# Delta rule: one is added to the gate's tanh, and the gate product is done on GpSimd instead of VectorE, with new step orders on all engines

## The reference, cut to what matters

```python
def step(S, inp):
    qt, kt, vt, at, bt = inp
    err = jnp.einsum('bhvk,bhk->bhv', S, kt) - vt
    S = at[..., None, None] * S - bt[..., None, None] * err[..., None] * kt[:, :, None, :]
    o = jnp.einsum('bhvk,bhk->bhv', S, qt)
    return (S, o)
...
o = (o - mu) * jax.lax.rsqrt(var + 1e-05) * ln_w + ln_b
g = jax.nn.sigmoid(x @ Wg).reshape(B, T, H, DV)
o = (o * g).reshape(B, T, H * DV)
return o @ Wo
```

## Time and profile before

| what | value |
|---|---|
| median of three runs | 1885.67 us (1882.06 to 1886.81) |
| the profiled execution | 1887.38 us, of which the span is 1885.6 us |
| TensorE busy | 1781.6 us, 94% of the span |
| VectorE busy | 1529.9 us, 81% |
| ScalarE busy | 1286.9 us, 68% |
| GpSimd busy | 941.3 us, 50% |
| mean granted TensorE clock | 0.977 of full speed |

### The profile page before, as it was taken

The page is one execution under the profiler, slowest core; times in us unless marked ns, Lnnn a source line. Parts: engine busy times, 40 slices in busy tenths (PEclk is TensorE's granted clock), DMA queues, the critical chain, the costliest instruction groups (busy, mean ns, idle before and its releaser), DMA issues.

```text
span 1885.6 us, 49242 instructions
## 1 busy us (share of the span) xinstructions
PE 1781.6 (94%) x19366; PEld 1315.9 (70%) x19366; DVE 1529.9 (81%) x2561; ACT 1286.9 (68%) x2850; POOL 941.3 (50%) x1890
## 2 busy tenths in 40 slices
PE   8889999999899889999999999999999999999687
PEld 4733333332688767888888888888888888887576
DVE  6699999993466567989989999899899898998455
ACT  2068888889342357778777777787777777777553
POOL 1134344445223244666566566666666566565233
PEclk9989999999899999999999999999999999999889
...
DMA packets 74133, 78.61 MB, mean 42 GB/s; under 512 B 13168, under 2 KB 60784, under 8 KB 73904
## 3 DMA queue, kind: packets, MB, share of 16 engines
...
## 4 chain that ended last, share of the span: by engine, by line
PE 38%; ACT 14%; DVE 9%; issue 4%; POOL 1%; POOLq 0%; ACTq 0%; DVEq 0%
PE ps L1530 10%; PE ps L1678 5%; PE ps L1560 4%; DVE d_acc L1833 3%; PE ps L1660 3%; ACT d_kq L1717 3%; ACT d_tt L1769 2%; PE ps L1648 2%; PE ps L1654 2%; PE ps L1630 2%; ACT d_acc L1701 2%; PE ps L1637 2%; DVE d_o_g L1910 2%; PE ps L2008 1%; ACT d_ty L1766 1%
## 5 line engine op out<-in xcount | busy, mean ns | idle before, releaser
L1833 DVE SCALAR_TENSOR_TENSOR d_acc<-ps,d_par,d_acc 128x1023 f32<-128x1023 f32 (+2 forms) x288 | 366.1, 1271 | 25.7 <-ACT d_acc L1701 25.5
L601 ACT ACTIVATE a_prob<-ps 128x512 f32<-128x512 f32 (+2 forms) x640 | 309.3, 563 | 99.1 <-PE ps L567 93.9
L1530 PE MATMUL ps<-x1p,d_wh 128*128 128x512 f32 x1024 | 358.7, 431 | 7.1 <-DVE d_acc L1833 7.1
L623 DVE TENSOR_REDUCE a_mx<-ps 128x2 f32<-128x1024 f32 (+2 forms) x320 | 336.5, 1112 | 34.9 <-PE ps L551 27.2
L1530 PE MATMUL ps<-x1p,d_wl 128*128 128x512 f32 x512 | 203.1, 397 | 0.0
L510 POOL TENSOR_SCALAR_AFFINE_SELECT a_prob<-a_prob 128x128 f32<-128x128 f32 (+1 forms) x384 | 125.2, 330 | 125.1 <-ACT a_prob L601 114.1
L567 PE MATMUL ps<-q,k 51*128 51x512 bf16 (+2 forms) x640 | 175.1, 365 | 2.5 <-ACT a_prob L601 0.9
L1701 ACT ACTIVATE d_acc<-ps,d_par 128x512 f32<-128x512 f32 x192 | 145.8, 776 | 42.5 <-PE ps L1530 40.4
L1530 PEld LDWEIGHTS ps<-x1p,d_wh 128*128 128x128 f32 x1024 | 161.1, 191 | 18.4 <-DVE d_acc L1833 8.1
L1785 ACT ACTIVATE d_w_sb<-ps 128x128 f32<-128x128 f32 x256 | 70.5, 275 | 144.9 <-PE ps L1648 144.2
L581 PE MATMUL ps<-a_prob,a_v 128*32 128x512 f32 (+3 forms) x1536 | 165.0, 502 | 0.4 <-POOL a_prob L510 0.2
...
## 6 DMA issues: line engine op xcount, KB each, us to landing
...
```

The costliest lines, as they stand in the source:

```text
L601: inc(nc.scalar.activation(prob[:, y % PB, g:g + heads, off:], ps[:, PLACE["st", n, x], 0:heads * w].rearrange("p (h c) -> p h c", c=w), A ...
L623: inc(nc.vector.tensor_reduce(out, ps[:, bank:bank + 2, 0:heads * w].rearrange("p r (h c) -> p r h c", c=w), AX.X, ALU.max, negate=True), ...
L1530: last = nc.tensor.matmul(ps[:, bank, :], wp[g][:, k, i, :], x(part), start=(k == 0 and j == 0), stop=(k == KE - 1 and j == 2))
L1833: inc(nc.vector.scalar_tensor_tensor(acc[i][:, d:T], taps[:, 0:T - d], par[p][:, 4 * i + j:4 * i + j + 1], acc[i][:, d:T], ALU.mult, ALU.a ...
```

## The change

VectorE's o_turn, one scalar_tensor_tensor that adds one to the tanh and multiplies, goes. GpSimd gets two steps for it: gate.h adds one to the tanh in place, o_turn.j multiplies. VectorE keeps an empty step begin, to which the hook of the last stage is tied. The four rows of ORDER are new.

```diff
-            ("gated", 2, 4), ("og_h", 2, 2), ("og_l", 2, 4), ("added", 4, 8),
+            ("og_h", 2, 2), ("og_l", 2, 4), ("added", 4, 8),
...
-            ("ss", 1, 0), ("eyeb", 1, 0), ("qg", 1, 0), ("solved", 2 * HB - 2, 0),
+            ("ss", 1, 0), ("gate", 2, 0), ("gated", 2, 4), ("eyeb", 1, 0), ("qg", 1, 0), ("solved", 2 * HB - 2, 0),
...
+        def gate_(n, h):
+            half_gate = gate[n % 2][:, h * HALF:(h + 1) * HALF]
+            W("graw", n, h + 1)
+            inc(nc.gpsimd.tensor_scalar(half_gate, half_gate, 1.0, None, ALU.add), "gate")
+
+        def o_turn(n, j):
+            c = slice(j * HALF, (j + 1) * HALF)
+            W("gate", n, j + 1)
+            W("affine", n, j + 1)
+            inc(nc.gpsimd.tensor_tensor(o_g[n % 2][:, c], o_g[n % 2][:, c], gate[n % 2][:, c], ALU.mult), "gated")
...
-        def o_turn(n, j):
-            W("affine", n, j + 1)
-            c = slice(j * HALF, (j + 1) * HALF)
-            inc(nc.vector.scalar_tensor_tensor(o_g[n % 2][:, c], gate[n % 2][:, c], 1.0, o_g[n % 2][:, c], ALU.add, ALU.mult), "gated")
+        def begin(n):
+            pass
...
-        if step == ("o_turn", 0):
+        if step == ("begin",):
```

Of the table, one row before and after:

```diff
     "POOL": """
-        S.solve.1 S.solve.2 S.solve.3 S.solve.4 S.qg X.og.0 L.scalars O.wo L.split O.stats X.og.1 L.solve.0""",
+        O.gate.0 X.wo S.solve.0 S.solve.1 S.solve.2 S.solve.3 S.solve.4 X.o_turn.0 X.o_turn.1 O.gate.1 X.og.0 X.og.1 L.split L.scalars O.stats S.qg""",
```

More of the change, by code:

```diff
@@ L1244 @@
     "PE": """
[L1245 to L1248, removed]
@@ L1249 @@
-        S.qs.4 S.s.4 S.pw.4 E.proj.1.0.0 S.ks.5 E.proj.1.0.1 S.w.5""",
+        O.pw.3 S.v_turn.0 O.ks.4 O.qs.4 X.o_turn.1 S.gate.0.0 O.w.4 S.gate.0.1 O.s.4 S.k_turn.0 O.pw.4 O.ks.5 L.proj.1.0.0 O.w.5 L.proj.1.0.1 O.qs.5
+        O.s.5 S.k_turn.1 O.pw.5 S.y32 L.proj.1.1.0 O.ks.6 S.z32 O.w.6 L.proj.1.1.1 O.qs.6 O.s.6 S.y64 O.pw.6 O.ks.7 X.out.0 S.z64 O.w.7 O.qs.7 X.out.1
+        O.pw.7 S.v_turn.1 S.y128 L.proj.2.0.0 L.proj.2.0.1 L.proj.2.1.0 L.proj.2.1.1 L.pair.0 S.z128 L.pair.1 S.w.0 L.pair.2 S.s.0 L.pair.3 S.pw.0
@@ L1250 @@
+        S.ks.1 X.out.2 S.w.1 O.o_turn.0 S.qs.1 S.pw.1 S.s.1 X.out.3 E.proj.0.0.0 S.ks.2 E.proj.0.0.1 S.qs.2 S.w.2 E.proj.0.1.0 S.s.2 E.proj.0.1.1
+        S.pw.2 S.ks.3 S.gate.1.0 S.w.3 S.gate.1.1 S.qs.3 S.s.3""",
     "ACT": """
-        O.w.1 S.blocks O.pw.1 O.w.2 L.tap.0.0 S.silu.2 L.tap.0.1 O.pw.2 O.w.3 X.norm.0 O.gate.1 O.pw.3 S.v_turn.0 O.w.4 X.norm.1 O.pw.4 O.w.5
-        X.o_turn.0 L.tap.1.0 O.pw.5 S.spread L.tap.1.1 O.w.6 S.y32 X.o_turn.1 S.v_turn.1 X.og.0 O.pw.6 S.diag O.w.7 S.y64 L.silu.0 S.z64 O.pw.7
@@ L1253 @@
-        L.silu.1 S.y128 L.tap.2.0 L.tap.2.1 S.gate.0 S.z128 S.w.0 S.pw.0 X.og.1""",
+        O.gate.0 X.w.6 S.tap.1.1 O.y64 X.pw.6 O.diag X.w.7 O.z64 X.pw.7 S.silu.0 S.silu.1 O.y128 S.tap.2.0 O.v_turn.1 S.tap.2.1 O.z128 O.w.0 X.norm.0
+        O.pw.0 O.w.1 S.blocks O.pw.1 X.norm.1 O.w.2 L.tap.0.0 S.silu.2 O.pw.2 L.tap.0.1 O.w.3 X.o_turn.0 O.pw.3 O.gate.1 S.v_turn.0 O.w.4 O.pw.4
+        X.o_turn.1 O.w.5 S.spread X.og.0 L.tap.1.0 S.y32 O.pw.5 X.og.1""",
     "DVE": """
-        O.s.5 O.pw.2 S.columns O.pw.3 O.ks.6 O.pw.4 S.turned X.o_turn.0 L.conv.1.0 O.s.6 S.whole O.ks.7 L.conv.1.1 O.pw.5 O.pw.6 L.conv.1.2 S.k_turn.0
@@ L1256 @@
-        S.k_turn.1 X.o_turn.1 O.pw.7 L.decay O.stats L.conv.2.0 L.pair.0 L.conv.2.1 S.s.0 L.pair.1 L.pair.2 S.ks.1 L.conv.2.2 L.pair.3 S.s.1 X.out.0
-        S.ks.2 S.pw.0 L.lanes S.s.2 X.out.1 S.ks.3 E.conv.0.0 S.s.3 E.conv.0.1 S.ks.4 E.conv.0.2 S.pw.1 S.s.4 X.out.2 S.ks.5 X.out.3""",
+        O.s.3 L.conv.0.1 O.ks.4 L.conv.0.2 O.s.4 O.pw.1 O.ks.5 S.columns S.k_turn.0 O.pw.2 S.k_turn.1 X.begin S.turned O.s.5 O.ks.6 S.whole O.pw.3
+        O.pw.4 O.pw.5 O.s.6 L.conv.1.0 O.ks.7 L.conv.1.1 O.pw.6 L.conv.1.2 X.out.0 O.pw.7 X.out.1 O.stats L.decay L.conv.2.0 L.pair.0 L.pair.1
@@ L1258 @@
+        L.conv.2.1 S.s.0 L.pair.2 S.ks.1 L.pair.3 L.conv.2.2 S.s.1 L.lanes S.ks.2 S.pw.0 X.out.2 S.s.2 S.ks.3 X.out.3 E.conv.0.0""",
     "POOL": """
-        S.solve.1 S.solve.2 S.solve.3 S.solve.4 S.qg X.og.0 L.scalars O.wo L.split O.stats X.og.1 L.solve.0""",
+        O.gate.0 X.wo S.solve.0 S.solve.1 S.solve.2 S.solve.3 S.solve.4 X.o_turn.0 X.o_turn.1 O.gate.1 X.og.0 X.og.1 L.split L.scalars O.stats S.qg""",
 }
@@ L1418, in gpsimd @@
         pool.sem_inc(SEM["nm"][0], 1)
+        pool.sem_inc(SEM["gated"][0], 4)
         pool.sem_inc(SEM["og_l"][0], 4)
@@ L1506, in gpsimd @@
         pool.wait_ge(c_made, 8)
-        E_.walk("POOL", {"scalars": scalars, "split": split, "qg": qg, "solve": solve, "stats": stats, "wo": wo_, "og": og})
+        E_.walk("POOL", {"scalars": scalars, "split": split, "qg": qg, "solve": solve, "stats": stats, "wo": wo_, "gate": gate_, "o_turn": o_turn, "og": og})
     def tensor(pe):
@@ L1819, in vector @@
         W = E_.wait
-        dve.sem_inc(SEM["gated"][0], 4)
         dve.sem_inc(SEM["added"][0], 8)
@@ L1920, in vector @@
         E_.walk("DVE", {"conv": conv, "decay": decay, "pair": pair, "k_turn": k_turn, "lanes": lanes, "columns": columns, "turned": turned, "whole": whole,
-                        "ks": ks, "s": s_, "pw": pw, "stats": stats, "o_turn": o_turn, "out": out})
+                        "ks": ks, "s": s_, "pw": pw, "stats": stats, "begin": begin, "out": out})
     return Programs(sync, gpsimd, tensor, scalar, vector), waits
```

## The result

The changed kernel takes 1909.21 us (median of 4 runs, 1908.85 to 1909.72) against 1886.09 (4 runs, 1882.06 to 1886.81): ratio 1.0126, 95% interval 1.0109 to 1.0142. It is 23 us slower, where 5 us faster was forecast. The profiled execution took 1909.72 us with a span of 1908.0, 22.4 more than before's.

What follows compares the result with a forecast made beforehand. TensorE was taken to bound the kernel, with stages of 34.3 us against 34.4: -3 us over 31 stages and -2 at the ends took 1887.4 to 1882.4, written as a median of 1881 us; range 1868 to 1896.

Steps and rivals of the forecast that it cites:

- 33.3 + 1.0 = 34.3 us: New stage: TensorE's own work plus its wait before ks.1 for the state copy, against 34.4 us before.
- Filling starts the same way: Pipeline's start: claimed to begin as before; no step of it was priced.
- The floor: TensorE's own work in a stage, 33.3 us, claimed unchanged because both tables hold the same TensorE steps.
- The gate product: GpSimd gains two products (1.28 us each) and two additions (0.8 each) a stage; throughput costs nothing, latency may.
- Rival C: GpSimd's product comes late and TensorE stands 0.5 us at z32: stage 34.8, 1896 us; chance 0.20.
- Point 1: ScalarE from y64's result: diag begins at 12.3, no waits for TensorE, tap.2.1 ends at 21.3 us.
- Point 2: VectorE from conv.2.0 to s.0: state ready at 25.2; TensorE wants it for ks.1 at 24.2, waits 1.0 us.
- Point 3: TensorE before pair.1: the wait for the gate's tanh goes, through another bank and z128 between the pairs.
- Point 4: From ks.1 to the next stage: GpSimd's additions and products covered by 0.4 us at z32, 2.1 at X.out.0.
- The ends: Drain and fill: last unit 2.3 us sooner, fill as before, the norm equal within 1 us; taken as -2 us.
- From pair.3 to w.0 the chain [...] is the same work: Drain, last unit: lanes, solve, columns and narrow steps claimed unchanged by the new order.

Runs made afterwards that it cites:

- The run with the waits filled: Changed kernel with two TensorE swaps: v_turn.1 ahead of pw.7, proj.2.0.0 ahead of y128; 1905.96 us, ratio 1.0107.
- the one with silu.1 cut: Changed kernel with TensorE's swaps before pw.7 and y128, plus ScalarE's silu.1 done for one chunk of eight from the third unit on; 1885.26 us, ratio 1.0002.
- the z128 runs: Old order with z128 moved between pair.0 and pair.1: 1882.11 us (0.9986) with addition and product on GpSimd, 1886.05 us (1.0004) with the product on VectorE.
- the run with gate.0 sooner: Old order with addition and product on GpSimd, ScalarE's gate.0 (the tanh) put ahead of tap.2.0; 1895.36 us, ratio 1.0050.

## Why the prediction was wrong

The step that failed is the sum of the stage, "33.3 + 1.0 = 34.3 us": both of its terms were too small, TensorE's own work and the time for which it waits for the chain. The trace shows 33.7 + 1.3 = 35.04 in their place. A second step failed beside it, "Filling starts the same way": 4.7 us were lost up to unit 4, of which, as an estimate, two stages longer by 0.63 make 1.3. The mechanism, a wait for the state at the end of the chain, was forecast rightly.

*What bounds the kernel.* Right in kind: TensorE, and its waits. The floor was to be 33.3; the new order without its 1.3 us of waits is 33.7. The forecast took an out step as 0.71, as many columns as a product group. It measures 0.80 with the step behind it, 0.09 more in each of the four, which is about the missing 0.4. From ks.1 to the stage's end, where two of them stand, it made 9.4 instead of 9.1.

*The gate product (first paragraph of the change).* The product was right at 1.28. The addition was wrong at 0.8 for 1.50, above even the bound of 1.28 that was put on it for reading less; it cost nothing. Rival C did not happen: line 1467 never took over 1.29 us, z32 did not wait.

*Point 1, the ScalarE row.* Y64 came at 11.17 for 11.1, but tap.2.1 ended at 21.69 for 21.3. Three spacings were summed too short: diag began 0.2 later than forecast, and where ScalarE goes from w.7 to z64 and from pw.7 to silu.0 the starts are 0.30 apart, not 0.17. The 0.17 came from the old order's rows, where other copies stand behind w.7 and silu.1 behind pw.7; what makes the difference isn't shown.

*Point 2, VectorE's block.* Right: 3.9 us from conv.2.0 to the state, and TensorE waits there and nowhere new. But it stated the wait at ks.1 as 1.0 us over a floor, and so hid what it hung on: the time of ks.1 is y64's plus the chain, 14.5 us and not 14.1, and TensorE's own speed between the two has no part in it as long as it gets there before the state. The run with the waits filled and the one with silu.1 cut show this.

*Point 3.* Right, the gate's wait is gone. What it is worth by itself was not measured: the z128 runs left the tanh and pair.1 where they were, and the run with gate.0 sooner removed the wait but made the state later, for a stage 0.33 longer.

*Point 4.* Right: no wait at z32 or X.out.0.

*The stage.* 35.04 against 34.3, cut along the loop: 0.4 from the chain (14.5 for 14.1), 0.3 from TensorE's path behind ks.1 (9.4 for 9.1), 0.07 from y64's place. These are the mis-sized terms; 31 times 0.7 us is the larger part of the 28 us between forecast and result. A forecast gain of 0.1 a stage was the difference of two sums with an error several times as large, so even its sign was not supported.

*The ends.* Forecast -2, measured +0.3 in the drain and +4.7 in the fill. In the drain the last unit's pair.3 was indeed sooner, 30.4 for 32.1 after its first group. What failed is "From pair.3 to w.0 the chain [...] is the same work": it took 31.2 us for 28.8. Lanes follow 5.0 instead of 4.1 behind pair.3, y32 14.0 instead of 12.6 behind lanes, and y128 5.5 instead of 5.0 behind y64; w.0 is at 61.5 for 60.9.

In the fill, for which no step was priced, the interval from unit 2 to 3 grew from 33.6 to 37.0. Busy times and TensorE's granted clock (the column behind POOL) in the changed kernel:

```profile
715.00:720.00 5.00, 3.34 (x75) 2.64 (x74) 3.81 (x10) 4.73 (x13) 1.40 (x2) 0.85 0.01 3
720.00:725.00 5.00, 5.00 (x17) 3.88 (x14) 2.72 (x8) 3.46 (x6) 4.76 (x5) 0.50 0.00 0
```

and in the one with the waits filled:

```profile
715.00:720.00 5.00, 3.95 (x33) 2.93 (x32) 3.40 (x13) 4.80 (x10) 2.63 (x4) 1.00 0.00 0
720.00:725.00 5.00, 4.78 (x36) 3.63 (x35) 3.89 (x4) 4.31 (x11) 4.84 (x4) 1.00 0.00 0
```

In the changed kernel TensorE had stood still for 1.48 us before pw.7 at 717.96, among shorter gaps; then its granted clock was 0.50 of full, the 1.2 GHz level, for these 5 us, and product groups followed each other in 1.28 us instead of 0.69. With the waits filled the clock stayed at 1.00 and the interval was 34.8. The new-order kernels without filled waits all had 36.9 to 37.0 there, those with them 34.0 to 34.8, and the old order 33.5 to 34.1. So 2.2 of the 3.4 us go with the lower clock. That the gaps brought the clock down is the reading of these pairs; it was not tried by itself.
